# Banded attention: probabilities divided by their sum before they are transposed, the mix written with channels on the partitions, and values projected one place earlier

## The reference

```python
qkv = jnp.einsum('bnd,ed->bne', x, w_qkv)          # x after a layer norm
q, k, v = jnp.split(qkv, 3, axis=-1)
...
q, k = _rope(q, k, offset=0)
valid = (j > i - WINDOW) & (j <= i)                 # WINDOW = 64
scores = jnp.einsum('bhnd,bhkd->bhnk', q, k) * scale
scores = jnp.where(valid[None, None], scores, -jnp.inf)
att = jax.nn.softmax(scores, axis=-1)
out = jnp.einsum('bhnk,bhkd->bhnd', att, v)
out = out.transpose(0, 2, 1, 3).reshape(Bq, Nq, INNER)
y = jnp.einsum('bni,di->bnd', out, w_o)
```

## Time and profile before

| what | us |
|---|---|
| median of three runs | 1907.24 |
| span of the profiled execution | 2028.0 |
| PE busy in that span | 1785.8 (88%) |
| DVE busy | 1312.5 (65%) |
| ACT busy | 804.2 (40%) |
| POOL busy | 797.0 (39%) |
| first `scores` to last `scores` of the banded attention | 986.25 to 1536.84 |

### The profile page before, as it was taken

How to read it: one execution, slowest core, us unless ns; L and a number is a source line. 1 busy time by engine, 2 the same in 40 slices (tenths; PEclk the granted TensorE clock), 3 DMA queues, 4 the chain that set the end, 5 groups by cost and what they waited for, 6 DMA issues and landing times. The chain is left out here.

```text
span 2028.0 us, 39275 instructions
## 1 busy us (share of the span) xinstructions
PE 1785.8 (88%) x14393; PEld 1508.3 (74%) x14393; DVE 1312.5 (65%) x2649; ACT 804.2 (40%) x1961; POOL 797.0 (39%) x1082
## 2 busy tenths in 40 slices
PE   5999999999999999984899999999996727588885
PEld 3888888888888888872688888888875516577773
DVE  5877787777777788877766666666764616233334
ACT  3444444444444444432455555555553202122221
POOL 3333533344333444433624324334342571145541
PEclk9999999999999999985999999999997758788886
DMA  2100010001960000001200101000002421644426
GB/s 92 48 0 0 0 48 0 0 0 51 348 4 0 1 1 0 0 0 37 74 1 1 43 1 43 1 1 2 2 2 82 173 105 40 174 134 145 153 100 236
DMA packets 72003, 108.83 MB, mean 54 GB/s; under 512 B 24096, under 2 KB 52640, under 8 KB 70976
## 3 DMA queue, kind: packets, MB, share of 16 engines
q1 hardware_dynamic: 61552, 77.59, 13.5%
q0 software_dynamic: 9168, 25.31, 3.2%
q10 hardware_dynamic: 1152, 4.19, 0.5%
HBM read 62.37 MB, written 44.96 MB: 53 GB/s over the span
## 5 line engine op out<-in xcount | busy, mean ns | idle before, releaser
L1820 POOL DMA_INDIRECT ys<-rows_yb,dest x127 | 122.2, 962 | 192.2 <-ACT rows_yb L2117 157.7
L846 POOL TENSOR_TENSOR a_ms<-a_ms,a_esq 128x4 f32<-128x4 f32 x64 | 14.4, 224 | 436.5 <-DVE a_ms L733 436.5
L1346 ACT ACTIVATE b_prob<-b_sc,b_nmax 128x128 f32<-128x128 f32 x256 | 99.8, 392 | 143.0 <-DVE b_nmax L1437 143.0
L1432 DVE SCALAR_TENSOR_TENSOR b_sc<-b_ps_s,window_mask 128x512 f32<-128x512 f32 x64 | 44.3, 692 | 121.6 <-PE b_ps_s L1225 121.6
L1199 PE MATMUL b_ps_u<-xh,b_w_hi 128*128 128x512 f32 x256 | 113.4, 443 | 3.1 <-DVE b_rope L1424 2.1
L602 DVE RECIPROCAL a_rz<-a_ps_sz 128x256 f32<-128x256 f32 x64 | 112.5, 1757 | 3.7 <-PE a_ps_sz L350 3.7
L2009 PE MATMUL t_ps<-t_wd,rows_hT 64*128 x256 | 79.4, 461 | 40.1 <-ACT rows_hT L2110 28.4
L561 ACT ACTIVATE a_sq<-a_ps_og 128x512 f32<-128x512 f32 x64 | 38.3, 598 | 176.3 <-PE a_ps_og L456 161.0
L1524 POOL TENSOR_TENSOR b_Q<-b_rope 128x512 f32<-128x512 f32 x32 | 41.2, 1287 | 161.6 <-DVE b_rope L1424 161.6
L1199 PE MATMUL b_ps_u<-xl,b_w_hi 128*128 128x512 f32 x256 | 101.5, 396 | 0.0
L1199 PE MATMUL b_ps_u<-xh,b_w_lo 128*128 128x512 f32 x256 | 101.2, 395 | 0.0
(11 more groups left out here) (352 smaller groups left out, 6150.7 us busy)
## 6 DMA issues: line engine op xcount, KB each, us to landing
xs<-a_zeros SPq DMA_DIRECT2D x32, 528.0 KB, 12.5
xn_all<-xs SPq DMA_DIRECT2D x32, 528.0 KB
wgu_all<-wgu SPq DMA_DIRECT2D x4, 2048.0 KB, 13.8
b_w_raw<-Wb SPq DMA_DIRECT2D x12, 512.0 KB, 5.0
wgu_all<-ys SPq DMA_DIRECT2D x8, 512.0 KB, 11.9
wgu_all<-ys ACTq DMA_DIRECT2D x8, 512.0 KB, 12.4
X<-x SPq DMA_DIRECT2D x2, 1024.0 KB, 7.0
a_w_raw<-Wv SPq DMA_DIRECT2D x4, 512.0 KB, 6.1
```

The lines of the kernel that those rows point to most:

```text
L1346: last = nc.scalar.activation(prob[:, n % 2, h, :], sc[:, h % 2, h // 2, :], ACT.Exp, bias=nmax[:, at:at + 1], accum_out=den[:, n % 2, 0, ...
L1820: pool.indirect_dma_start(ys, bass.IndirectOffsetOnAxis(ap=dest[:, i % HOMES, j:j + 1], axis=0), yb[:, i % YR, j // 2, j % 2, :], None).th ...
```

## The change

The division by the sum of the exponentials moves from the mix's result to the probabilities: `prob_norm(n)` multiplies `prob` by the inverse of `den` in place, in SBUF, before `turn_prob(n)` transposes it. `mix` swaps its operands: a half of a head's value channels is the stationary operand and 64 tokens of `pT` are the moving one, so `ps_m` comes out with channels on the partitions. `o_norm`, `turn_o` and the tile `o` go; `o_high` and `o_low` read the mix's result itself. On PE `project_v(n+1)` goes ahead of `turn_prob(n-1)`. On DVE `rotate(.., 1)` of the unit before and `add_y(n-2)` go between `mask_max(n)` and `inverse(n)` in every step.

```diff
             def turn_prob(n):
-                pe.wait_ge(exp_out, n + 1)
+                pe.wait_ge(prob_out, n + 1)
...
                     for e, v in enumerate((Vs[:, n % VSR, :], V[:, n % VR, :])):
                         q = slice(e * WIN, (e + 1) * WIN)
-                        last = nc.tensor.matmul(ps_m[q, h * DH:(h + 1) * DH], pT[:, h, q],
-                                                v[:, h * DH:(h + 1) * DH], start=True, stop=True)
+                        for d in range(2):
+                            rows = slice(d * WIN, (d + 1) * WIN)
+                            last = nc.tensor.matmul(ps_m[rows, h * P + e * WIN:h * P + (e + 1) * WIN],
+                                                    v[:, h * DH + d * WIN:h * DH + (d + 1) * WIN], pT[:, h, q],
+                                                    start=True, stop=True)
                 last.then_inc(p_m, 1)
-
-            def turn_o(n):
-                pe.wait_ge(on_out, n + 1)
-                for h in range(GH):
-                    last = nc.tensor.transpose(ps_m[:, h * P:(h + 1) * P], o[:, h, :], ident)
-                last.then_inc(p_ot, 1)
...
             for n in range(N + 1):
+                if n + 1 < N:
+                    project_v(n + 1)
                 if n:
                     turn_prob(n - 1)
-                if n + 1 < N:
-                    project_v(n + 1)
...
                 if n + AHEAD < N:
                     unit(n + AHEAD, 0)
-                if n:
-                    turn_o(n - 1)
                 if n + AHEAD < N:
                     unit(n + AHEAD, 1)
...
             def o_high(n):
-                act.wait_ge(p_ot, n + 1)
+                act.wait_ge(p_m, n + 1)
...
-            def o_norm(n):
-                dve.wait_ge(p_m, n + 1)
+            def prob_norm(n):
                 dve.wait_ge(inv_out, n + 1)
-                after(dve, p_ot, n - 1)
-                nc.vector.tensor_tensor(o[:], c3(ps_m[:]), den[:, n % 2, 1, :].unsqueeze(2).broadcast_to([P, GH, DH]),
-                                        ALU.mult).then_inc(on_out, 1)
+                nc.vector.tensor_tensor(prob[:, n % 2, :, :], prob[:, n % 2, :, :],
+                                        den[:, n % 2, 1, :].unsqueeze(2).broadcast_to([P, GH, SEEN]),
+                                        ALU.mult).then_inc(prob_out, 1)
...
                 if n < N:
                     mask_max(n)
-                if 2 <= n < FILLING:
+                if n and n - 1 + AHEAD < N:
+                    rotate(n - 1 + AHEAD, 1)
+                if n >= 2:
                     add_y(n - 2)
-                if n:
-                    o_norm(n - 1)
                 if n < N:
                     inverse(n)
+                    prob_norm(n)
                 if n + AHEAD < N:
                     rotate(n + AHEAD, 0)
                 if n:
                     o_low(n - 1)
                 if n >= LAST + 3:
                     normalise_out(n - LAST - 3)
-                if n >= FILLING:
-                    add_y(n - 2)
-                if n + AHEAD < N:
-                    rotate(n + AHEAD, 1)
```

More of the change, by code:

```diff
@@ L1117, in window_stage @@
         pT = sb("pT", [P, GH, P])
-        o = sb("o", [P, GH, DH])
         oT_hi, oT_lo = sb("oT_hi", [P, GH, P], F32R), sb("oT_lo", [P, GH, P], F32R)
@@ L1134, in window_stage @@
         v_high, v_low, wo_high, wo_low = (sem(n) for n in ("v_high", "v_low", "wo_high", "wo_low"))
[L1135 to L1138, removed]
+        p_u, u_read, rot, p_v, p_s, p_pt, p_m, p_y = (
+            sem(n) for n in ("p_u", "u_read", "rot", "p_v", "p_s", "p_pt", "p_m", "p_y"))
+        masked, maxed, exp_out, inv_out, prob_out, pt_out, v_out, o_hi, o_lo, y_add = (
+            sem(n) for n in ("masked", "maxed", "exp_out", "inv_out", "prob_out", "pt_out", "v_out", "o_hi",
                              "o_lo", "y_add"))
@@ L1396, in _ @@
                     high_wo(g + 1)
-        FILLING = 6
         @block.vector
```

## The result

The changed kernel takes 1928.57 us (median of four runs, 1927.58 to 1929.67), the kernel before, beside it, 1906.39 (four runs, 1903.50 to 1908.77): a ratio of 1.0115, 95% interval 1.0103 to 1.0127. It is slower by 22.2 us, where 22.9 were forecast.

What follows compares the result with a forecast made beforehand. PE's list bounded the kernel before, at 8.75 us a step; with DVE the new bound, 55 x 0.43 + 13 x 0.25 = +26.9, less 4.0 at the ends, gives +22.9: 1930.1 us, range 1911 to 1942 (8 of 10).

Steps and rivals of the forecast that it cites:

- the hold: On DVE, `prob_norm` waits for a sum of POOL's `combine` and ends at 5.69 instead of 5.20, 0.49 us lost.
- one sum and not both: Only POOL's first sum holds `prob_norm`; the rival, held by both, had 1997.8 us and chance 0.05.
- `o_low` as the new bound: DVE's list from scores to `o_low` sets the step: 9.18 us, or 9.43 with the K copy, against 8.75.
- the upper bound of 1.90: Rival on PE: `mix` pays for every instruction, 1.90 us and not 1.12; 1935.6 us in all, chance 0.05.
- the unhindered list of PE: PE's own work per step without waits: `turn_o` out saves 0.35 us, `mix` adds 0.1, `project_v`'s order nothing.
- the fresh start of the second half: On PE, the unit's second half no longer starts afresh without `turn_o`: about 0.1 us more saved, not counted.
- the stall in the unit: PE's second half of the unit waits for the early rotate, starting at 3.85 instead of 3.68: 0.17 us.
- the rival "not held": `prob_norm` runs in 0.68 us beside `combine`, PE decides, step 8.67, time 1898.8 us; chance 0.11.
- the ends: Start and end of the stage, outside the 55 steps: -1.5 us at the start and -2.5 at the end.
- late `combine`: One step without units at the end of the stage is lengthened by a late `combine`: +0.4 us.
- The last result: End of the stage: saves `o_norm`, `turn_o` and two handovers less `prob_norm`, some 2 us (an estimate).
- `project_v` moved at no price and no gain: On PE, the same ten matmuls ahead of `turn_prob` cost nothing as long as `turn_prob` is not waiting.

Runs made afterwards that it cites:

- e1: Changed kernel with GpSimd's `combine` also waiting for the same step's `prob_norm`: 1900.9 us, 0.9962 of before.
- e2: Changed kernel with `o_low` put ahead of the step's first rotate, right behind `prob_norm`: 1898.2 us, 0.9953 of before.
- e5: Changed kernel with `o_low` right behind `prob_norm` and the second rotate at the end of VectorE's step: 1880.7 us, 0.9868 of before.
- b0: The kernel before, unchanged, profiled a second time: steps 4 to 59 take 481.15 us in both profiles.
- e4: Changed kernel with only `project_v` put back behind `turn_prob`: 1942.0 us, 1.0180 of before.
- e7: The kernel of e5 with `project_v` put back behind `turn_prob`: 1907.8 us, 1.0004 of before.
- e6: The kernel of e5 with the second rotate early again in the first four steps only: 1876.3 us, 0.9835 of before.

## Why the prediction came out

*Right: the hold, its place and its size.* The working gave 1.17 us for `prob_norm` (1.18 measured), one sum and not both, `o_low` as the new bound, `out_project` at 7.56 (7.58), a step of 9.18 (9.16 to 9.19, and 9.40 to 9.44 with the K copy), 26.9 us for the 55 steps (27.2). e1 shows that POOL's sum is the cause in 46 of the 55 steps, e2 that it counts through `o_low` only. In the last nine the statistics make DVE's list too long even without a hold (9.06, e1). The working has no statistics in it; that its 9.18 fits these steps as well is luck, as `prob_norm` starts later there and still ends behind the same sum. The instance of another kernel stage carried over to the tenth. The Trainium skill, "SBUF — State Buffer", section "Who interferes with whom", says that a DVE instruction with two inputs in SBUF contends with a GpSimd instruction that reads SBUF, and that whoever issues first keeps the other out until it is done. The traces agree: `prob_norm` 1.18 beside a sum and 0.69 in e1, while `o_low`, with one input from PSUM, keeps 0.68 beside a sum.

*Right: `mix`.* From its start to the unit's is 1204.41 - 1203.33 = 1.08 us, against the 1.12 taken and the upper bound of 1.90. The Trainium skill (TensorEngine Tiling (Array Packing), section Instruction Overhead) gives each matmul some 60 cycles and puts one of a single column level with one of 60. That does not make 1.90: these have 64 columns, so by it two of them cost about what one of 128 does (an estimate from that page). The trace agrees: 1.08 us for `mix` against 1.02 before.

*Mis-sized: the unhindered list of PE.* The text counted 0.35 less for `turn_o`, 0.1 more for `mix` and nothing for the order of `project_v`, and left the fresh start of the second half out of the sum. By e5 the list is 0.48 shorter: 8.27. Piece by piece, median starts in before and in e5: `turn_o` -0.35, the unit 2.99 to 2.84 (-0.15), `project_v`, which no longer follows four transposes, 1.475 to 1.364 (-0.11), `out_project`, which now does, 1.52 to 1.60 (+0.08), `mix` 1.02 to 1.08 (+0.06). Therefore the stall in the unit is not 0.17 but about 0.38 (the unit is 3.22 long in the median, 2.84 in e5). This did not show in the forecast, since both nearly cancel, by luck: with a shorter list and a longer stall PE comes at 7.07 (e2, mean of the middle steps) in place of 7.15, and waits for `o_low` in either case. By the same luck the rival "not held" had the right size, 8.67, against 8.69 in the 46 steps of e1: there, too, PE is near 7.1 when `o_low` ends. Its time, 1898.8 against 1900.9, leaves out the nine steps of 9.06.

*Mis-sized: the ends.* The first steps give 1.6 back (1.5 forecast), but the steps without units and what follows, to the end of the stage, give 4.1 and not 2.5, and two errors lie in that. The four steps from 59 to 63 were to give 0.5 and cost 0.8 (31.9 against 31.1 us). The first is 0.4 longer by its late `combine`, as forecast, and two go from 7.79 to 7.50 (forecast 7.48). But the last one takes 8.73: in it there is no `project_v` left ahead of `turn_prob`, and PE waits longer and then goes on at a granted clock of 0.58.

```profile
1563.54 0.65 PE L1232 MATMUL b_ps_t<-square_consts,b_prob 128*128 128x128 f32 x4 [3.07 <-DVE b_prob L1437]
```

```profile
1563.54:1567.01 3.47, 3.47 (x17) 3.04 (x17) 0.86 (x2) 0.59 (x1) 0.73 (x1) 0.58 0.00 0
```

The last result, from the last `scores` to the end of the stage, was estimated to save 2 and saves 4.8 (19.8 to 15.0 us). 1.3 of that is the last `out_project`, which takes 2.97 us to `add_y` at a granted clock of 0.50 before (b0) and 1.70 at 1.00 after. The working has no term for the clock; that the two errors are of opposite sign is luck.

*Wrong in part: `project_v` moved at no price and no gain.* In a middle step of the changed kernel that holds (e4). But it keeps 8.5 us out of the last steps, by the estimate above more through PE's clock than through its own time, and 0.38 us out of each step once PE is the bound (e7), because the division put DVE between the exponentials and `turn_prob`.

So the change as made had a shorter list for PE, 55 x 0.48 = 26 us, and lost 53 us of its own order of DVE: 0.38 a step by the early rotate, and about 0.5 by `o_low` behind the held instruction, a little more with the K copy.

## What to carry to other kernels

When an instruction with both inputs in SBUF is added to VectorE, look at what GpSimd runs at that moment, and start GpSimd's work behind it or put what another engine waits for directly after it. An instruction moved forward on one engine also moves what it releases: here an early rotate cost more through the sums that it set off, and through the buffer that it read late, than through its own time. A move that is free while another engine is the bound can be worth several per cent of a step when that bound is lifted, so test it again on the final order. And where PE has little else to do, work that fills a wait can count twice: its own time, and the clock that PE goes on with.

## What the runs showed of the hardware

- The hold goes both ways. While `prob_norm` streams, POOL's second sum, already started, takes 1.74 us in place of 1.28; in e1, without the meeting, it is 1.28 again.
- A matmul group that follows four transposes takes longer: `project_v` 1.475 us from start to start behind them (before; 1.472 in e7) and 1.364 without (e5), `out_project` 1.60 (e5) and 1.52 (before; 1.51 in e7).
- PE, after 5.5 us with little work at the start of e5, ran at a granted clock of 0.50 in the 6.50 us that follow; in e6, without that pause, it stayed at 1.00 (from 989 to 1012 us). In the last steps PE went on at 0.65 after it had been busy for 2.19 of 5.26 us (e4), and at 1.00 after 3.76 of 5.26 (the changed kernel).
- 32 records of 128x64 stationary and 64 moving columns take 1.08 us from start to start, 16 of 128x64 with 128 moving columns 1.02: half the columns cost about half as much for each record.
